# A fixed table of places for every step of a two-layer transformer kernel, in place of a list scheduler

## The reference

```python
x = L0_attn_x                                   # (4, 1024, 128)
xn = _layernorm(x)
x = x + _L0_attn_ref(xn, ...) + _L0_ffn_ref(xn, ...)
xn = _layernorm(x)
x = x + _L1_attn_ref(xn, ...) + _L1_ffn_ref(xn, ...)
```

## Time and profile before

| | us |
|---|---|
| three runs | 1503.05, 1503.81, 1507.08 |
| their median | 1503.81 |
| the profiled execution's span | 1503.8 |
| PE busy | 1395.6 (93%) |
| PE weight loads | 990.6 (66%) |
| DVE busy | 1250.3 (83%) |
| ACT busy | 1042.7 (69%) |
| POOL busy | 360.9 (24%) |
| DMA bytes | 238.02 MB, mean 158 GB/s |

### The profile page before, as it was taken

One profiled execution on the slowest core, in us unless ns is written; L12 is line 12 of the kernel. 1 busy time (PEld: TensorE's weight loads), 2 busy tenths in 40 slices (PEclk: granted clock), 3 DMA queues, 4 the chain that ended last, 5 costly groups with the idle time before them and its releaser, 6 DMA issues.

```text
span 1503.8 us, 20880 instructions
## 1 busy us (share of the span) xinstructions
PE 1395.6 (93%) x6198; PEld 990.6 (66%) x6198; DVE 1250.3 (83%) x1511; ACT 1042.7 (69%) x2411; POOL 360.9 (24%) x251
## 2 busy tenths in 40 slices
PE   6999999999899999899999899999889999999858
PEld 4677766666566666566665667656677677777636
DVE  3344467877999989999959897999999999999996
ACT  6455757676886777766877768777857787776652
POOL 0001203110221402011131411131543353344410
PEclk9999999999999999999999999999999999999989
DMA  7763445335544554533363335355555556555244
GB/s 270 261 255 139 157 146 185 118 114 168 167 135 148 179 164 135 206 117 111 109 216 113 99 107 168 121 155 174 162 184 167 158 176 198 162 174 160 86 112 155
DMA packets 111243, 238.02 MB, mean 158 GB/s; under 512 B 13207, under 2 KB 52844, under 8 KB 109644
## 3 DMA queue, kind: packets, MB, share of 16 engines
q1 hardware_dynamic: 106588, 227.31, 47.9%
q0 software_dynamic: 4544, 9.38, 1.8%
HBM read 185.59 MB, written 43.86 MB: 153 GB/s over the span
## 4 chain that ended last, share of the span: by engine, by line
PE 44%; issue 20%; DVE 16%; ACT 9%; POOL 8%; DMA 2%; SPq 0%; ACTq 0%; POOLq 0%; DVEq 0%
PE bank L1363 8%; PE bank L1351 7%; PE bank L1353 6%; PE bank L1352 6%; POOL RSTD L1025 4%; PE bank L1543 3%; DVE AM L1087 3%; POOL ytok L1040 3%; ACT ROWS L865 2%; PE bank L1458 2%; DVE SH L1217 2%; DVE TA L1083 2%; PE bank L1452 1%; ACT ROWS L878 1%; DVE TA L1092 1%
## 5 line engine op out<-in xcount | busy, mean ns | idle before, releaser
L1025 POOL TENSOR_TENSOR RSTD<-SS,power_half 128x4 f32<-128x4 f32 x96 | 158.8, 1654 | 816.7 <-ACT ROWS L865 816.5
L1363 PE MATMUL bank<-SH,WD 128*128 128x512 f32 x512 | 263.6, 596 | 0.8 <-DVE X L1233 0.8
L1351 PE MATMUL bank<-NH,GU 128*128 128x512 f32 x512 | 245.5, 479 | 2.0 <-DMA GU<-halves 1.0
L1217 DVE TENSOR_TENSOR SH<-SH,bank 128x512 f32<-128x512 f32 x256 | 172.4, 682 | 76.4 <-ACT SH L853 46.4
L1087 DVE TENSOR_TENSOR AM<-AM,TA 128x1024 f32<-128x1024 f32 x192 | 230.2, 1219 | 0.9
L1083 DVE TENSOR_TENSOR TA<-QKV 128x2048 f32<-128x2048 f32 x96 | 219.5, 2287 | 1.2
L1353 PE MATMUL bank<-NL,GU 128*128 128x512 f32 x512 | 203.0, 397 | 0.0
L1352 PE MATMUL bank<-NH,GU 128*128 128x512 f32 x512 | 202.6, 396 | 0.0
L853 ACT ACTIVATE SH<-bank 128x512 f32<-128x512 f32 x256 | 153.1, 605 | 59.6 <-PE bank L1353 57.5
L878 ACT ACTIVATE ROWS<-bank,RSTD 128x128 f32<-128x128 f32 x384 | 110.0, 374 | 56.2 <-POOL RSTD L1025 50.8
L1578 PE MATMUL bank<-XT,GU 128*128 128x256 f32 x624 | 147.5, 381 | 0.3 <-DVE SH L1335 0.3
(11 more groups left out here) (232 smaller groups left out, 2764.8 us busy)
## 6 DMA issues: line engine op xcount, KB each, us to landing
GU<-halves SPq DMA_DIRECT2D x112, 512.0 KB, 4.2
QKV<-QKV SPq DMA_DIRECT2D x32, 720.0 KB
GU<-in_w_gu SPq DMA_DIRECT2D x39, 512.0 KB, 3.6
xg<-in_c_fill SPq DMA_DIRECT2D x8, 2080.0 KB
WD<-in_w_d SPq DMA_DIRECT2D x128, 128.0 KB, 2.2
FC<-ready_w SPq DMA_DIRECT2D x32, 512.0 KB, 5.2
WQ<-ready_w SPq DMA_DIRECT2D x32, 384.0 KB, 4.8
WD<-in_w_d SPq DMA_DIRECT2D x39, 256.0 KB, 3.8
```

The source lines that it names most:

```text
L1025: pool.tensor_tensor(RSTD[:], SS[:], (power_one if k[0] == "at" else power_half)[:], ALU.pow).then_inc(power_done, 1)
L1217: dve.tensor_tensor(SH[:, g % 4, :], SH[:, g % 4, :], banks[2 + g % 2][:], ALU.mult).then_inc(h_ready, 1)
L1351: pe.matmul(out, w_hi, x_hi, start=True, stop=False)
L1363: pe.matmul(banks[4][:], WD1[:, slot, :], SH[:, g % 4, :], start=first, stop=last).then_inc(down_done, 1)
```

## The change

`Plan`, `TUNE`, the urgencies and `schedule()`'s description of steps go. A table `PLACES` gives, for each step name and engine, the place of every key in that engine's order; `step_keys()` lists the keys in the order in which the table's numbers stand, and `TAKES_PART` says which keys have a part on an engine. `schedule()` sorts by the places and derives the rest: the order of keys within a name, and which half of `QKV` a tile's layer uses. Every engine gets the same steps as before, with the same instructions. The lines behind the new text are moved by 215 (L826 is L1041).

```diff
-class Plan:
...
-    def run(self):
...
-                    rank = (max(at, now + self.READY), urgency)
...
-TUNE = {
-    "early": 162.28,
...
+PLACES = {
...
+    "fill": {
+        "SP": (31, 32, 48, 69, 101, 132, 167, 202,),
+    },
...
+TAKES_PART = {
...
+    ("normed", "ACT"): lambda key: key[0] in ("n0", "n1", "n3", "A", "C"),
+    ("normed", "DVE"): lambda key: key[0] != "n3",
...
 def schedule():
-    plan = Plan()
-    step = plan.step
...
+    every, at = step_keys(), {}
+    for name, engines in PLACES.items():
+        for engine, places in engines.items():
+            mine = [key for key in every[name] if TAKES_PART.get((name, engine), lambda key: True)(key)]
...
+            for key, place in zip(mine, places):
+                at.setdefault(engine, {})[place] = (name, key)
+    orders = {engine: [steps[i] for i in sorted(steps)] for engine, steps in at.items()}
...
+    return orders, keys, half_of
...
-    sums_before = count_before("ACT", ("keys_exp", "query"), lambda name, key: name == "scale" and key[0] == "at")
+    sums_before = count_before("DVE", ("keys_exp", "query"), lambda name, key: name == "normed" and key[0] == "at")
```

More of the change, by code:

```diff
@@ L161 @@
-TUNE = {
-    "early": 162.28,
[L163 to L179, removed]
-}
@@ new lines, in schedule @@
+def schedule():
+    every, at = step_keys(), {}
+    for name, engines in PLACES.items():
+        for engine, places in engines.items():
+            mine = [key for key in every[name] if TAKES_PART.get((name, engine), lambda key: True)(key)]
+            assert len(mine) == len(places), (name, engine, len(mine), len(places))
+            for key, place in zip(mine, places):
+                at.setdefault(engine, {})[place] = (name, key)
+    orders = {engine: [steps[i] for i in sorted(steps)] for engine, steps in at.items()}
+    assert all(sorted(steps) == list(range(len(steps))) for steps in at.values())
+    keys = {}
+    for name, engines in PLACES.items():
+        per_engine = [[key for n, key in orders[engine] if n == name] for engine in engines]
+        longest = max(per_engine, key=len)
+        if name == "normed":
+            longest = keys["turn"]
+        elif name == "route":
+            longest = [(t, i) for t, last in longest if last == 3 for i in range(4)]
+        assert all([key for key in longest if key in some] == some for some in per_engine), name
+        keys[name] = longest
+    halves, half_of = list(range(HALVES)), {}
+    freed = [key[0:2] for name, key in orders["DVE"] if name == "ham" and key[2] == HAM + 1]
+    for i, key in enumerate(key[0:2] for name, key in orders["ACT"] if name == "views" and key[2] == 0):
+        half_of[key] = i if i < HALVES else half_of[freed[i - HALVES]]
+    return orders, keys, half_of
```

550 lines of the change are left out of this document (369 added, 181 removed), and 129 rows, old and new, of the table PLACES.

## The result

The changed kernel takes 1514.99 us, the median of five runs (1513.11 to 1522.95), beside 1504.54 us of the kernel before (1503.05 to 1507.08, five runs). The ratio is 1.0069, with a 95% interval of 1.0045 to 1.0092. It is slower, by 10.4 us, where 13 us less was forecast, and outside the range, which ended at 1511. The profiled execution has a span of 1512.4 us; that of before had 1503.8.

The account below looks back on a forecast made before the run. It took TensorE to bound the kernel, with VectorE close behind from 220 us and the bound from 1400 to 1478. The sum: 1503.8 − 6.7 − 1.75 − 3.2 − 4.3 − 5 − 2 + 10.4 = 1491.2 us; range 1474 to 1511.

Parts of the forecast that it names:

- (i): Shifted semaphore wait for the exponentials costs nothing; other loads, moved a few places, were issued 30 us or more before use.
- last sign of being wrong: A new long wait at a place the prediction hadn't named would upset the forecast as a whole.
- (g): Second tile's fill right behind the first's delays a `keep` near 72 us; TensorE loses 7.0 plus 3.4 of clock, +10.4 us.
- (a): 788 to 793 us: TensorE's 3.30 us wait for bank 6 and 3.4 of lost clock go, −6.7 us.
- (a) to (d): TensorE waits near 408, 568, 700, 757, 788 to 793 and 993 us go or shrink, with lost clock; together −16.0 us.
- third rival: Waits move: filled gaps reopen elsewhere through the one scaling bank, a third to two thirds goes; 1500 to 1507, chance 0.17.
- (e): 1050 to 1400 us: three TensorE waits given work in front; a bit over a third of 13.2 passes, −5 us.
- (f): The end, 1400 to 1478 us: the last tile's additions move ahead of merges that aren't urgent, −2 us.
- (h): End of SP's queue: loads of last results now precede the last `roll`; taken as 0, bounds 0 and +13 us.
- slower rival: VectorE's `ham` chain, 220 to 1400 us, sets the pace; some 3 of 23 us pass, fill is paid: 1511, chance 0.16.

Follow-up runs that it names:

- e5_queue_mid: Changed kernel with SP's places 104 to 133 in the old order and the mlp weights of (3,0) ahead of tile 6's fill; 0.9942 of the kernel before.
- e8_before_queue: Kernel before with the second tile's fill behind visit 18 and the mlp weights of (3,0) ahead of tile 6's fill; 0.9981 of the kernel before.
- e7_before_fill: Kernel before with one edit, the second tile's fill directly behind the first tile's; 1.0063 of the kernel before, 9.5 us more.
- e6_fill_late: e5_queue_mid with the second tile's fill moved behind the weight load of visit 18, near 120 us; 1485.7 us, 0.9866 of the kernel before.
- e9_early_only: e6_fill_late with the kernel before's order on all five engines from the first gate_up on, some 1020 us; 0.9865 of the kernel before.
- e1_fill_back: Changed kernel with only the second tile's fill back at its old place in SP's queue, 16 places ahead; 1.0044 of the kernel before.

## Why the prediction was wrong

**The step that failed is (i)**: "Other loads are moved by up to a few places and were issued 30 us or more before use." It put these moves at nothing. The 30 us don't hold for the q weights of (0,2): they were issued 20 us before their use at 411.85, and had 15 us between landing and use. Two places were enough: they went behind `roll (2,0)`, for which SP waits 16.0 us, and a `visit`, and were issued 19 us later. The projection weights had 36 us, and went ten places back, behind a fill. Two rolls went back by 8 and 4. e5_queue_mid measured these places, with the mlp weights of (3,0), at 19 us. The mlp weights stood badly in the kernel before as well, where moving them together with the fill gave 3 us (e8_before_queue); that leaves some 16 for what the change did. I had priced them at 0 and didn't list them: the queue that I did follow place by place was only the piece around the fills. The prediction's last sign of being wrong, a new long wait at a place that it hadn't named, is what came.

**(g), the fill, was right in cause and size, and not in its path.** 10.4 forecast, 9.5 measured alone (e7_before_fill), 11 in the changed kernel (e5_queue_mid to e6_fill_late). The `keep` took 9.0 us longer to land than before, 9.9 had been worked out. The Trainium skill's rule (page "DMA: Bandwidth & Descriptors", section "Why a DMA increments its semaphore by 16 and not by 1", that such transfers share the lowest-numbered engines) agrees with this trace in that the two fills share engines: 28.6 us for 19.6. Which engines they are, no row shows. The path was the other one: TensorE stopped for the down weights (6.21 us in e7_before_fill), which the prediction had at 6 us and didn't add, and not for the chain over ScalarE. The clock was priced too high, since a stretch of half clock that begins inside the wait costs only half of what is worked in it: 2.0 us at 101 us in the changed kernel and 1.9 in e7_before_fill, for the 3.4 that were taken. At (a) it is 3.0 for 3.4, by the 5.91 us worked.

**(a) to (d), −16.0, came out at −7.6**, by one trace of each kernel. Between e8_before_queue and e6_fill_late, the ends of the same `expert` steps move by −2.3 us at 790 (forecast −6.7), −1.9 around 410 (−1.75), −1.6 at 993 (−3.2), nothing at 568, −1.0 at 700 and −0.8 at 757 (−4.3 for the three). The reason at (a) is in the trace of e6_fill_late:

```profile
778.01 0.50 PE L1630 MATMUL bank<-NH,GU 128*128 128x512 f32 x1 [1.80 <-DVE SH L1496]
...
787.26 0.38 PE L1731 MATMUL bank<-centre,attn_raw 128*128 128x128 f32 x1 [1.22 <-DVE XSL L1535]
```

The wait of 3.30 us and its half clock are gone, and two waits of 1.80 and 1.22 stand in the next steps. The third rival said this, of a third to two thirds; it was right for these parts, and its total was too low because it didn't look at the queue.

**Two gains weren't seen.** By the same steps 4.4 us come between 34 and 45 us, and 6.5 in smaller pieces elsewhere up to 1006 us, where the prediction named nothing. The first is shown by the windows view of the kernel before and of e6_fill_late:

```profile
34.40:37.80 3.40, 3.40 (x10) 2.67 (x10) 0.77 (x2) 3.30 (x6) 0.00 (x0) 0.50 0.77 330
20.00:60.00 40.00, 38.60 (x166) 27.61 (x164) 17.81 (x27) 26.74 (x43) 0.56 (x1) 0.96 0.73 279
```

```profile
20.00:60.00 40.00, 39.87 (x177) 28.33 (x176) 17.52 (x28) 25.91 (x45) 1.01 (x1) 1.00 0.78 291
```

TensorE waited 1.4 us, until 32.71, and then had 3.4 us of half clock, together 3.1 of the 4.4 us; the new order has neither. Where the rest comes from isn't shown. So the early orders gave 17 us in all where 16 was forecast, and less than half of it came from the named places: the total was right by accident.

**(e) and (f), −7, gave nothing that was measured** (e9_early_only). Traces have 2.5 to 5 us: the changed kernel's lag falls from 13.1 us at 1006 to 8.3 at 1410. I had let a third of (e) pass; with VectorE at 335.0 of 350 us a value nearer the bound of 0 was the better choice. **(h)** was taken at 0, and that held: the first load of results is issued at 1448.66 us in the changed kernel, the last roll at 1455.35, 12 us later than before, and the products that need it begin at 1464.91 with no wait in front. The one wait of VectorE over 1 us in the 10 us before them, 1.27, is for TensorE.

**The slower rival** had the number, 1511, but not the reason. It put the loss on VectorE's chain, which swallows TensorE's gains. The level stretches between the waits speak against it up to 1050 us, and so do e5_queue_mid, whose gain at the waits near 418 to 650 us came through whole (the steps' ends have 19.3 us of it from 400 to 660, the ratios 19), and e6_fill_late:

```profile
0.00:220.00 220.00, 207.90 (x901) 148.34 (x902) 100.11 (x167) 131.66 (x290) 20.76 (x25) 1.00 0.60 209
220.00:1050.00 830.00, 788.79 (x3294) 532.55 (x3293) 747.34 (x941) 615.18 (x1444) 174.78 (x118) 1.00 0.48 148
1050.00:1400.00 350.00, 331.59 (x1730) 261.41 (x1729) 338.09 (x344) 255.70 (x595) 153.02 (x99) 1.00 0.56 169
1400.00:1478.00 78.00, 59.83 (x269) 39.67 (x268) 61.78 (x60) 31.64 (x80) 12.93 (x10) 0.87 0.44 129
```

VectorE is busy 747.34 of the 830 us from 220 on, more than the 734.2 of the earlier trace rows, and TensorE 788.79: the two gain together. After 1050 the rival may hold: no gain was measured there.

As a sum, in ratios to the kernel before: engines' orders −0.0115, the mlp weights and the fill's late place −0.0019, the fill beside the other +0.0076, loads and rolls (and the mlp weights back in their old place) +0.0127 makes 1.0069. It closes by construction, each term being the difference of two neighbouring kernels, and each carries some 0.003 but the second, with 0.0015.

## What to carry to other kernels

Follow every moved transfer, not only the large ones: for each take its issue, its landing and its use from the trace, and ask what stands ahead of it now that waits. A load's spare time is lost in one step when it goes behind an issue that waits for data or a free slot, or behind a long copy, however few places that is. Here the waits that were filled with other work gave about half of their price in all, and at (a) the trace shows new waits a step later; those that were taken away at their source, in the queue, gave nearly all.

## What the runs showed of the hardware

A small transfer issued closely behind a DRAM-to-DRAM copy of 8 outer rows is held up by about the length of the copy, 9.9 us as estimated from the earlier trace rows, though such a copy alone keeps only half of the DMA engines busy: 64 KB took 13.7 us right behind one and 1.7 without, 256 KB took 11.8 issued 3.9 us behind one, and 1024 KB took 28.6 behind two and 19.6 behind one. Other loads are under way at these places, so no row shows a copy's share alone.

A stretch of half clock can begin inside the wait that goes with it, and its length isn't in proportion to the wait: 10.2 us with 8.96, of which 3.97 were worked, 6.8 with 6.21 (3.78 worked), 3.4 with both 3.88 and 3.83 (all of it worked), and 10.2 again with a wait of 3.35 us in the changed kernel, of which 7.7 were worked:

```profile
863.00:873.20 10.20, 7.71 (x27) 6.68 (x28) 7.75 (x8) 6.28 (x15) 8.94 (x6) 0.50 0.19 64
```

So the price of a wait is its length and half of the time worked at half clock. That sum gives 11.0 us for the fill's stall in the changed kernel, 8.1 in e7_before_fill and 8.5 in e1_fill_back, where the ends of the `expert` steps move by 10.8, 8.3 and 8.5.

Executions of e6_fill_late and e9_early_only, whose orders are the same up to 1020 us, stand 3.9 us apart at 1006 us, as much as many of the terms here; a term of that size needs repeated runs, not one trace.
